# A running state formed in 128x32 column tiles and applied in 32x32 array tiles, with a new written order of steps

## The chip, the core and the metric

The program runs on one core of a Trainium2 chip. TensorE multiplies matrices (PE in the profile, its weight loads PEld), VectorE is DVE, ScalarE is ACT, GpSimd is POOL, and the DMA queues are issued from SP and POOL. The metric is the device time of one launch in microseconds (us), as the median of several runs. Profiled times are of one execution.

## The reference

A batch of 32 rows of 256 tokens goes through three stages. The first is a two-layer tower of width 128 with 8 heads of 16 (below). Its output of width 256 then goes through an attention without softmax (16 heads of 64) and a gated MLP of 768, each added to its input.

```python
# one layer of the tower; H=8 heads, HD=16
q, k, v = (layernorm(x) @ w + b, split into heads); k = k / sqrt(HD)
k, v = causal_conv(filters, k), causal_conv(filters, v)
Z = einsum('bhsd,bhse->bhsde', v, k)
gates = relu(Z.reshape(.., HD*HD) @ gk + gb)**2 + EPS
attn = cumsum(gates * Z, axis=2) / (cumsum(gates, axis=2) + EPS)
o = einsum('bhsd,bhsde->bhse', q, attn); o = o / max(norm(o), EPS)
x = x + o @ ok + ob
x = x + gelu(layernorm(x) @ ff1 + b1) @ ff2 + b2
```

The sum over positions of `gates * Z` is, for each head, a 16x16 matrix that grows along the sequence: v transposed times (gate times k). The kernel cuts the 256 positions into two halves of 128. The second half needs that matrix summed over the whole first half. This is "the running state" here.

## The kernel before, in words

Two batch rows make a group, so there are 16 groups. The tower treats four groups at a time (streams 0 to 3), each in its own buffers, shifted in time against each other, so that a new group enters while three are at later steps. The rest (attention and MLP, called B here) has two streams.

Nothing is looped on the chip: `PLACES_A`, `STARTS_A`, `PLACES_B`, `STARTS_B` and `PREPARE` give every step a number (its place plus the start of its group), all steps are sorted by that number, and each engine issues its own steps in that order and in no other. A step that waits on a semaphore holds all later steps of its engine. The numbers are keys of an order, not times; two groups of the tower stand about 1001 apart. A step is (name, layer or LN number, part); for example `("kv", 1, 0, ...)` is the first half of the keys and values of the second layer. Steps of later groups stand among those of earlier ones.

The attention of one layer of the tower, for one group, in the order of its data:

- `kv`, `conv`, `turn_v`, `gate`: TensorE makes keys and values, convolves them, transposes the values and multiplies them with the gate weights. DVE takes `kv` out (L587) and multiplies in `gate_mul` (L597).
- `gated` (DVE, L605 to L616): sums, bias, square, and at last `gk`, the keys times their gates, laid out in blocks of two heads.
- `state` (PE): for each batch row b, a product of all 128 columns of `vc` (the stationary side) with all 128 columns of the gated keys (L837), 128x128 results of which only the 16x16 blocks on the diagonal are wanted; then two small products with `causal` and `ones` for the sums of the gates (L841, L843). All go into one PSUM bank.
- `state_low` (DVE, L625 to L629): the floor of the norm, and `state`, which is the 128x256 result times `same_head`, a 0/1 matrix that keeps the diagonal blocks.
- `qk` (PE, L856) and `mask` (DVE, L638): the scores in four banks for each pair of positions blocks, times `causal`.
- `av` (PE), parts 0 to 3: the scores with the gated keys, 8 matmuls in 128x32 column tiles (L878). Parts 2 and 3 belong to the second half and first multiply `state` with the queries (L870), one full 128x128 matmul each.
- `norm` (ACT), `sum` (PE, L889), `chain` (DVE, L647 to L665), `unit` (PE, L897), `unit_out` (DVE, L672), `wo` (PE, L903) and `wo_out` (DVE, L678) normalise and project. `f1`, `gelu`, `f2`, `f2_out` are the feed-forward part (L753 to L755, L748, L919, L684).

A layer norm is `stats` (DVE, L562, L567, and L570, the variance), `pow` (POOL, L509), `shift` (DVE, L575), `xn` (ACT, L709), `turn` (PE, L789), `high` (ACT) and `low` (DVE, L581). POOL also does `bias` (x plus the bias of the next projection, L514), `embed` (L504) and `gather` (L479).

A float32 matmul of the program shows as two MATMUL instructions (and two LDWEIGHTS) in the trace. PSUM banks are handed out in the order in which the sorted steps claim them, a ring of 8 in the tower.

Of the kernel before, what the change touches and what calls it, by code (L numbers as in the profile page):

```python
# [10 lines left out]
ALU = mybir.AluOpType  # L11
# [24 lines left out]
PLACES_A = [("embed", 0, 0, 335), ("stats", 0, 0, 506), ("pow", 0, 0, 630), ("shift", 0, 0, 680), ("xn", 0, 0, 757),  # L36
            ("turn", 0, 0, 592), ("high", 0, 0, 809), ("low", 0, 0, 822), ("bias", 0, 0, 1024), ("q", 0, 0, 941),
            ("q_out", 0, 0, 1183), ("kv", 0, 0, 763), ("kv_out", 0, 0, 881), ("kv", 0, 1, 771),
            ("kv_out", 0, 1, 883), ("conv", 0, 0, 841), ("conv_out", 0, 0, 932), ("conv", 0, 1, 859),
            ("conv_out", 0, 1, 945), ("turn_v", 0, 0, 895), ("vT_out", 0, 0, 1131), ("gate", 0, 0, 992),  # L40
            ("gate_mul", 0, 0, 1284), ("gated", 0, 0, 1354), ("state", 0, 0, 1246), ("state_low", 0, 0, 1467),
            ("qk", 0, 0, 960), ("mask", 0, 0, 961), ("qk", 0, 1, 1198), ("mask", 0, 1, 1450), ("av", 0, 0, 1248),
            ("av", 0, 1, 1311), ("av", 0, 2, 1314), ("av", 0, 3, 1336), ("norm", 0, 0, 1583), ("sum", 0, 0, 1399),
            ("chain", 0, 0, 1684), ("unit", 0, 0, 1481), ("unit_out", 0, 0, 1773), ("wo", 0, 0, 1661),
            ("wo_out", 0, 0, 1842), ("stats", 1, 0, 1853), ("pow", 1, 0, 1993), ("shift", 1, 0, 1903),
            ("xn", 1, 0, 1895), ("turn", 1, 0, 1883), ("high", 1, 0, 2048), ("low", 1, 0, 1945),
            ("bias", 1, 0, 2176), ("f1", 0, 0, 1954), ("gelu", 0, 0, 2248), ("f1", 0, 1, 1956), ("gelu", 0, 1, 2271),
            ("f1", 0, 2, 2017), ("gelu", 0, 2, 2359), ("f1", 0, 3, 2060), ("gelu", 0, 3, 2434), ("f2", 0, 0, 2130),
            ("f2", 0, 1, 2151), ("f2", 0, 2, 2212), ("f2", 0, 3, 2229), ("f2_out", 0, 0, 2474),
            ("stats", 2, 0, 2483), ("pow", 2, 0, 2563), ("shift", 2, 0, 2652), ("xn", 2, 0, 2602),  # L50
            ("turn", 2, 0, 2451), ("high", 2, 0, 2720), ("low", 2, 0, 2701), ("bias", 2, 0, 2993), ("q", 1, 0, 2710),
            ("q_out", 1, 0, 2866), ("kv", 1, 0, 2487), ("kv_out", 1, 0, 2731), ("kv", 1, 1, 2587),
            ("kv_out", 1, 1, 2758), ("conv", 1, 0, 2628), ("conv_out", 1, 0, 2764), ("conv", 1, 1, 2633),
            ("conv_out", 1, 1, 2822), ("turn_v", 1, 0, 2673), ("vT_out", 1, 0, 2830), ("gate", 1, 0, 2823),
            ("gate_mul", 1, 0, 2897), ("gated", 1, 0, 2917), ("state", 1, 0, 2891), ("state_low", 1, 0, 2926),
            ("qk", 1, 0, 2838), ("mask", 1, 0, 2911), ("qk", 1, 1, 2872), ("mask", 1, 1, 2920), ("av", 1, 0, 2892),
            ("av", 1, 1, 2894), ("av", 1, 2, 2919), ("av", 1, 3, 2936), ("norm", 1, 0, 3130), ("sum", 1, 0, 2950),
            ("chain", 1, 0, 2959), ("unit", 1, 0, 3035), ("unit_out", 1, 0, 2984), ("wo", 1, 0, 3076),
            ("wo_out", 1, 0, 3312), ("stats", 3, 0, 3338), ("pow", 3, 0, 3337), ("shift", 3, 0, 3444),
            ("xn", 3, 0, 3526), ("turn", 3, 0, 3283), ("high", 3, 0, 3531), ("low", 3, 0, 3483),  # L60
            ("bias", 3, 0, 3772), ("f1", 1, 0, 3358), ("gelu", 1, 0, 3591), ("f1", 1, 1, 3361), ("gelu", 1, 1, 3680),
            ("f1", 1, 2, 3403), ("gelu", 1, 2, 3709), ("f1", 1, 3, 3441), ("gelu", 1, 3, 3758), ("f2", 1, 0, 3414),
            ("f2", 1, 1, 3468), ("f2", 1, 2, 3480), ("f2", 1, 3, 3626), ("f2_out", 1, 0, 3801),
            ("stats", 4, 0, 3801), ("pow", 4, 0, 3781), ("shift", 4, 0, 3854), ("xn", 4, 0, 3882),
            ("turn", 4, 0, 3882), ("high", 4, 0, 3991), ("low", 4, 0, 3934), ("head", 0, 0, 3942),
            ("head_out", 0, 0, 3957), ("head", 0, 1, 3983), ("head_out", 0, 1, 3994), ("idx", 0, 0, 1577),
            ("gather", 0, 0, 1897), ("gather", 0, 1, 1993), ("gather", 0, 2, 3512), ("gather", 0, 3, 3925),
            ("store", 0, 0, 3837)]
STARTS_A = [434, 1435, 2438, 3441, 4443, 5445, 6445, 7448, 8448, 9448, 10450, 11450, 12454, 13455, 14458, 15457]
PLACES_B = [("b_load", 0, 0, 485), ("b_stats", 0, 0, 411), ("b_pow", 0, 0, 346), ("b_xn", 0, 0, 510),  # L70
            ("b_turn", 0, 0, 1053), ("b_high", 0, 0, 1144), ("b_low", 0, 0, 1023), ("b_turn", 0, 1, 1119),
            ("b_high", 0, 1, 1209), ("b_low", 0, 1, 1075), ("rows_high", 0, 0, 429), ("rows_low", 0, 0, 578),
            ("gram", 0, 0, 658), ("gram_high", 0, 0, 787), ("gram_low", 0, 0, 787), ("gram", 1, 0, 723),
            ("gram_high", 1, 0, 887), ("gram_low", 1, 0, 809), ("t1", 0, 0, 760), ("t1_even", 0, 0, 869),
            ("t1_odd", 0, 0, 812), ("t1", 0, 1, 763), ("t1_even", 0, 1, 919), ("t1_odd", 0, 1, 845),
            ("keys", 0, 0, 826), ("keys_out", 0, 0, 947), ("keys", 0, 1, 834), ("keys_out", 0, 1, 974),
            ("r", 0, 0, 988), ("r_high", 0, 0, 1007), ("r_low", 0, 0, 976), ("r", 0, 1, 1015),
            ("r_high", 0, 1, 1059), ("r_low", 0, 1, 1016), ("m", 0, 0, 1036), ("m", 0, 1, 1041), ("m", 0, 2, 1054),
            ("m_high", 0, 0, 1164), ("m_low", 0, 0, 1034), ("attn", 0, 0, 1144), ("attn_out", 0, 0, 1129),
            ("t1", 1, 0, 844), ("t1_even", 1, 0, 1014), ("t1_odd", 1, 0, 941), ("t1", 1, 1, 1000),  # L80
            ("t1_even", 1, 1, 1038), ("t1_odd", 1, 1, 977), ("keys", 1, 0, 1017), ("keys_out", 1, 0, 1119),
            ("keys", 1, 1, 1023), ("keys_out", 1, 1, 1147), ("r", 1, 0, 1060), ("r_high", 1, 0, 1164),
            ("r_low", 1, 0, 1053), ("r", 1, 1, 1097), ("r_high", 1, 1, 1167), ("r_low", 1, 1, 1071),
            ("m", 1, 0, 1126), ("m", 1, 1, 1131), ("m", 1, 2, 1135), ("m_high", 1, 0, 1223), ("m_low", 1, 0, 1107),
            ("attn", 1, 0, 1165), ("attn_out", 1, 0, 1132), ("b_stats", 1, 0, 1143), ("b_pow", 1, 0, 1156),
            ("b_xn", 1, 0, 1210), ("b_turn", 1, 0, 1211), ("b_high", 1, 0, 1367), ("b_low", 1, 0, 1213),
            ("b_turn", 1, 1, 1222), ("b_high", 1, 1, 1380), ("b_low", 1, 1, 1218), ("b_gate", 0, 0, 1515),
            ("b_up", 0, 0, 1624), ("silu", 0, 0, 1724), ("hid", 0, 0, 1744), ("hid_high", 0, 0, 1812),
            ("hid_low", 0, 0, 1923), ("b_gate", 1, 0, 1576), ("b_up", 1, 0, 1728), ("silu", 1, 0, 1780),
            ("hid", 1, 0, 1769), ("hid_high", 1, 0, 1849), ("hid_low", 1, 0, 2004), ("b_gate", 2, 0, 1583),  # L90
            ("b_up", 2, 0, 1762), ("silu", 2, 0, 1791), ("hid", 2, 0, 1955), ("hid_high", 2, 0, 2438),
            ("hid_low", 2, 0, 2057), ("b_gate", 3, 0, 1634), ("b_up", 3, 0, 1843), ("silu", 3, 0, 2001),
            ("hid", 3, 0, 2018), ("hid_high", 3, 0, 2491), ("hid_low", 3, 0, 2077), ("b_gate", 4, 0, 1767),
            ("b_up", 4, 0, 2432), ("silu", 4, 0, 2072), ("hid", 4, 0, 2436), ("hid_high", 4, 0, 2494),
            ("hid_low", 4, 0, 2435), ("b_gate", 5, 0, 1862), ("b_up", 5, 0, 2436), ("silu", 5, 0, 2076),
            ("hid", 5, 0, 2439), ("hid_high", 5, 0, 2498), ("hid_low", 5, 0, 2449), ("down", 0, 0, 2368),
            ("down", 1, 0, 2406), ("down", 2, 0, 2440), ("down", 3, 0, 2447), ("down", 4, 0, 2492),
            ("down", 5, 0, 2499), ("add", 0, 0, 2485), ("add", 1, 0, 2486), ("send", 0, 0, 2488)]
# [130 lines left out]
def token_tower(nc, semaphores, a, h_rows):  # L229
# [1296 lines left out]
```

## Time and profile before

| | us |
|---|---|
| median of 3 runs (lowest, highest) | 2023.23 (2022.75, 2024.51) |
| the profiled execution's own time | 2023.51 |
| its span | 2021.6 |

| engine | busy us | share of the span |
|---|---|---|
| PE | 1854.7 | 92% |
| PEld | 1586.4 | 78% |
| DVE | 1183.7 | 59% |
| ACT | 723.1 | 36% |
| POOL | 443.7 | 22% |

The busy time of PE is modelled, as matmuls are pipelined. In a timeline the first number of a row is the start in us from the start of the span, the second how long the merged instructions took together, "x16" how many they are, and in brackets stands for how long the engine was idle before and who ended that. The tower fills the span up to some 960 us, and B the rest.

### The profile page before, as it was taken

The numbers are of one execution on the slowest core, as the hardware profiler recorded it, in microseconds if no ns is written. First come the engines' busy times: TensorE is split into PE (matmuls) and PEld (weight loads), VectorE is DVE, ScalarE is ACT, GpSimd is POOL, SyncE is SP. The second block draws the span as 40 slices with busy tenths as digits, with TensorE's granted clock in tenths as the row PEclk, the third lists the DMA queues.
The fourth block names the chain that finished last, engine by engine and source line by source line (L and its number), as shares of the span: only waits on it lengthen the run. The fifth ranks groups of instructions, "written<-read, shape, count | busy, mean of one in ns | idle before, by whom it ended". The sixth has DMA issues, their size and how long they took to land.

```text
span 2021.6 us, 41920 instructions
## 1 busy us (share of the span) xinstructions
PE 1854.7 (92%) x17154; PEld 1586.4 (78%) x17154; DVE 1183.7 (59%) x3021; ACT 723.1 (36%) x1448; POOL 443.7 (22%) x393
## 2 busy tenths in 40 slices
PE   2689999999999999977899999999999999999998
PEld 1477778787778788866788888888888888888887
DVE  1468888888888888765644444344344444444443
ACT  1244444444444444442333222322232223222232
POOL 3213333332323222111111221122112211121112
PEclk8789999999999999987899999999999999999999
DMA  4000000000000000002100000000000000000000
GB/s 94 7 4 7 17 17 17 17 18 17 17 16 17 16 14 12 12 32 92 60 2 22 22 22 3 20 22 22 16 7 22 22 22 1 22 22 22 1 22 21
DMA packets 28699, 42.45 MB, mean 21 GB/s; under 512 B 6240, under 2 KB 22112, under 8 KB 28512
## 3 DMA queue, kind: packets, MB, share of 16 engines
q1 hardware_dynamic: 26464, 35.59, 5.5%
q0 software_dynamic: 2048, 4.20, 0.8%
q8 instruction: 138, 2.26, 0.5%
q14 instruction: 49, 0.40, 0.1%
HBM read 23.00 MB, written 16.78 MB: 20 GB/s over the span
## 4 chain that ended last, share of the span: by engine, by line
PE 57%; DVE 28%; issue 6%; POOL 3%; DMA 3%; SPq 1%; ACT 1%; DVEq 0%; POOLq 0%; ACTq 0%
PE ps L1314 11%; PE ps L1316 10%; PE ps L1315 10%; DVE att L638 5%; PE ps L1364 3%; PE ps L1380 3%; DMA h<-h_rows 3%; DVE bxn L1179 3%; PE ps L753 2%; DVE stats L562 2%; DVE bstats L1163 2%; PE ps L811 2%; PE ps L903 2%; PE ps L755 2%; PE ps L754 2%
## 5 line engine op out<-in xcount | busy, mean ns | idle before, releaser
L1153 POOL TENSOR_TENSOR hids_low<-hid,hids_high 128x512 fp32r<-128x512 f32 x96 | 137.8, 1442 | 606.1 <-ACT hids_high L1300 606.0
L509 POOL TENSOR_TENSOR rstd<-var,minus_half 128x4 f32<-128x4 f32 x80 | 83.2, 1040 | 607.0 <-DVE var L570 605.9
L709 ACT ACTIVATE xn<-x,shift,rstd 128x128 f32<-128x128 f32 x320 | 131.6, 484 | 163.0 <-DVE shift L575 162.9
L638 DVE TENSOR_TENSOR att<-ps,causal 128x512 f32<-128x512 f32 x256 | 158.3, 678 | 14.5 <-PE ps L856 14.5
L1314 PE MATMUL ps<-r_high,wq_high 128*128 128x256 f32 x512 | 148.9, 291 | 0.7 <-issue 0.7
L1316 PE MATMUL ps<-r_high,wq_low 128*128 128x256 f32 x512 | 144.8, 283 | 0.0
L1315 PE MATMUL ps<-r_low,wq_high 128*128 128x256 f32 x512 | 144.8, 283 | 0.0
L919 PE MATMUL ps<-w_f,wide 128*128 128x128 f32 x1024 | 130.0, 278 | 0.1
L919 PEld LDWEIGHTS ps<-w_f,wide 128*128 128x128 f32 x1024 | 122.2, 193 | 6.4 <-issue 5.0
L1300 ACT ACTIVATE hids_high<-hid 128x512 fp32r<-128x512 f32 x96 | 59.8, 630 | 146.8 <-PE ps L1316 134.6
L1314 PE MATMUL ps<-wd_high,hids_high 128*128 128x256 f32 x384 | 111.3, 290 | 0.7 <-POOL hids_low L1153 0.7
L1294 ACT ACTIVATE silu<-ps 128x512 f32<-128x512 f32 x96 | 55.4, 596 | 155.3 <-DVE hid L1229 86.3
L1315 PE MATMUL ps<-wd_low,hids_high 128*128 128x256 f32 x384 | 108.5, 283 | 0.0
L1316 PE MATMUL ps<-wd_high,hids_low 128*128 128x256 f32 x384 | 108.5, 283 | 0.0
L748 ACT ACTIVATE wide<-ps,b_f 128x512 f32<-128x512 f32 x128 | 84.5, 685 | 59.8 <-PE ps L755 59.8
L1202 DVE COPY t<-ps 128x512 f32<-128x512 f32 x64 | 44.1, 689 | 104.8 <-PE ps L1316 104.8
L1314 PE MATMUL ps<-wv_high,gram_high 128*128 128x512 f32 x256 | 105.0, 410 | 0.2 <-issue 0.2
L1210 DVE TENSOR_TENSOR r_low<-ps,r_high 128x512 fp32r<-128x512 f32 x128 | 80.9, 684 | 38.4 <-ACT r_high L1278 38.4
L1278 ACT ACTIVATE r_high<-ps 128x512 fp32r<-128x512 f32 x128 | 67.8, 599 | 97.1 <-PE ps L1380 97.1
L1315 PE MATMUL ps<-wv_low,gram_high 128*128 128x512 f32 x256 | 100.1, 391 | 0.0
L1316 PE MATMUL ps<-wv_high,gram_low 128*128 128x512 f32 x256 | 99.8, 390 | 0.0
L1185 DVE TENSOR_TENSOR bxT_low<-ps,bxT_high 128x512 fp32r<-128x512 f32 x64 | 42.8, 689 | 97.2 <-ACT bxT_high L1251 97.2
(354 smaller groups left out, 5055.3 us busy)
## 6 DMA issues: line engine op xcount, KB each, us to landing
h_rows<-h_out SPq DMA_DIRECT2D x16, 512.0 KB, 2.6
h<-h_rows SPq DMA_DIRECT2D x16, 512.0 KB, 3.9
out<-bxn SPq DMA_DIRECT2D x32, 256.0 KB, 2.5
att<-in_filters SPq DMA_DIRECT2D x1, 1024.0 KB, 7.0
emb<-in_embed,idx POOLq DMA_INDIRECT x64
stage<-in_W_vT SPq DMA_DIRECT2D x2, 512.0 KB, 4.8
wo<-in_W_oT SPq DMA_DIRECT2D x1, 1024.0 KB, 6.4
stage<-in_W_q SPq DMA_DIRECT2D x2, 512.0 KB, 6.8
```

The lines of the kernel that those rows point to most:

```text
L509: pool.tensor_tensor(rstd[s][:], var[s][:], minus_half[:], ALU.pow)\
L638: dve.tensor_tensor(masked[:, :, PAIR * g:PAIR * g + PAIR, :], bank("qk", s, l, j, g, t)[:].rearrange("p (n r t) -> p n r t", n=2, r=PAIR) ...
L709: act.activation(xn[s][:, j, :], x[s][:, j, :], ACT.Identity, bias=shift[s][:, j:j + 1], scale=rstd[s][:, j:j + 1]).then_inc(xn_made[s].se ...
L748: act.activation(gl[s][:, j, :], bank("f1", s, l, j, t)[:], ACT.Gelu_apprx_tanh, bias=b_f1[:, l, j:j + 1]).then_inc(gl_made[s].sem, 1)
L919: ins = pe.matmul(out[:, D * j:D * j + D], gl[s][:, f, P * j:P * j + P], w_f2[l][:, f, :], start=(f == 0 and j == 0), stop=(f == FC - 1), ...
L1153: pool.tensor_tensor(hids[1][:, halves, :], hid[:, half, :], hids[0][:, halves, :].bitcast(F32), ALU.subtract).then_inc(hid_low[s].sem, 1)
L1179: ins = dve.tensor_scalar(xn[s][:, j, :], h[s][:, j, :], mv[s][:, j, 0:1], rstd[s][:, j:j + 1], ALU.subtract, ALU.mult)
L1210: dve.tensor_tensor(low, bank("r", s, b, k, t)[:], high.bitcast(F32), ALU.subtract)\
L1278: act.activation(r[0][:, 2 * k:2 * k + 2, :].rearrange("p k n -> p (k n)"), bank("r", s, b, k, t)[:], ACT.Copy).then_inc(r_high[s].sem, 1)
L1314: pe.matmul(out, lhsT[0], rhs[0], start=start, stop=False, **kw)
L1315: pe.matmul(out, lhsT[0], rhs[1], start=False, stop=False, **kw)
L1316: return pe.matmul(out, lhsT[1], rhs[0], start=False, stop=stop, **kw)
```

## The change

The state bank shrinks: for each batch row it holds 128x32 results in place of 128x128. Row block q (partitions 32q to 32q+31, two heads) gets its own 128x32 column tile, with the 32 gated columns of the same two heads, so that only the blocks near the diagonal are formed. The mask is now `parity`, which tells the even head of a pair from the odd. The two gate sums come first in `state`. Where the state is applied, four matmuls in 32x32 array tiles stand in place of one of 128x128.

```diff
-    state = each("state", [P, NB, D])
+    state = each("state", [P, NB, BLOCK])
...
-            dve.tensor_tensor(state[s][:], bank("state", s, l, t)[:, 0:NB * D].rearrange(
-                "p (b d) -> p b d", b=NB), same_head[:].unsqueeze(1).to_broadcast([P, NB, D]),
-                ALU.mult).then_inc(g.sem, 1)
+            dve.tensor_tensor(state[s][:].rearrange("p b (r e) -> p b r e", r=PAIR),
+                              bank("state", s, l, t)[:, 0:NB * BLOCK].rearrange("p (b r e) -> p b r e", b=NB, r=PAIR),
+                              parity[:].unsqueeze(1).unsqueeze(3).to_broadcast([P, NB, PAIR, HD]),
+                              ALU.mult).then_inc(g.sem, 1)
...
-            for b in range(NB):
-                pe.matmul(out[:, D * b:D * b + D], vc[s][:, b, :],
-                          heads[:, PAIRS_A * b:PAIRS_A * b + PAIRS_A], start=(b == 0),
-                          stop=True, skip_group_check=True)
-            z, w = NB * D, NB * HEADS
-            pe.matmul(out[:, z:z + 2 * w], causal[:], gate[s][:], start=False, stop=False,
+            z, w = NB * BLOCK, NB * HEADS
+            pe.matmul(out[:, z:z + 2 * w], causal[:], gate[s][:], start=True, stop=False,
                       skip_group_check=True)
             pe.matmul(out[:, z + w:z + 2 * w], ones[:], gate[s][:, 0:w], start=False, stop=True,
-                      skip_group_check=True).then_inc(p_gate[s].sem, 1)
+                      skip_group_check=True)
+            for b in range(NB):
+                for q in range(PAIRS_A):
+                    rows = slice(BLOCK * q, BLOCK * q + BLOCK)
+                    ins = pe.matmul(out[rows, BLOCK * b:BLOCK * b + BLOCK], vc[s][:, b, rows],
+                                    heads[:, PAIRS_A * b + q], start=True, stop=True, skip_group_check=True)
+            ins.then_inc(p_gate[s].sem, 1)
...
-                pe.matmul(out, state[s][:, b, :], qT_last[s][:, P * b:P * b + P], start=True, stop=False,
-                          skip_group_check=True)
+                for q in range(PAIRS_A):
+                    rows = slice(BLOCK * q, BLOCK * q + BLOCK)
+                    pe.matmul(out[rows, :], state[s][rows, b, :], qT_last[s][rows, P * b:P * b + P], start=True,
+                              stop=False, skip_group_check=True)
```

All five order tables are written anew as well. Most steps keep their neighbours. The keys that change an order inside the repeating part of the tower, before and after (groups 1001 apart before, about 1004 after; a step of a group that entered n groups later adds n times that):

| step | before | after |
|---|---|---|
| `state` 1 and `av` 1,0 | 2891, 2892 | 2917, 2906 |
| `pow` 1, `bias` 2 | 1993, 2993 | 1969, 3047 |
| `bias` 1, `pow` 3, `embed` | 2176, 3337, 335 | 2176, 3119, 314 |
| `bias` 0 | 1024 | 1499 |
| `gate_mul` 1, `shift` 4, `shift` 1 | 2897, 3854, 1903 | 2926, 3918, 1918 |
| `chain` 0, `shift` 0 | 1684, 680 | 1704, 703 |
| `unit` 0, `kv` 1,0 and 1,1, `turn` 0 | 1481, 2487, 2587, 592 | 1654, 2628, 2629, 643 |
| `gate` 0, `f1` 0,2, `unit` 1 | 992, 2017, 3035 | 1092, 2054, 3093 |
| `av` 0,1 and `turn` 3 | 1311, 3283 | 1334, 3352 |
| `norm` 1 and `vT_out` 0 (ACT) | 3130, 1131 | 3196, 1160 |

In B, `b_gate` and `b_up` alternate earlier, `hid_low` 0 comes ahead of `b_pow` and `rows_high` of the next group, and `b_turn` 0 comes ahead of the second half of `keys`. In `PREPARE`, `wk_load` and the first `w_high` and `w_low` come earlier.

## Rows read from the trace of the kernel before

**Rows 1.** Stretches of the span: length, busy time of each engine, clock, DMA.

```profile
100.00:840.00 740.00, 697.07 (x7474) 587.40 (x7470) 614.23 (x1812) 351.86 (x745) 210.42 (x199) 0.99 0.05 15
840.00:1000.00 160.00, 127.77 (x1101) 106.95 (x1102) 93.52 (x247) 58.54 (x112) 19.57 (x17) 0.86 0.17 58
1000.00:2021.00 1021.00, 989.06 (x8293) 860.10 (x8291) 447.76 (x864) 295.38 (x554) 183.37 (x141) 1.00 0.05 17
```

**Rows 2.** Who waited for whom, PE alone, 100 to 850 us.

```profile
PE ps L837 <- DVE gk L616: 19.8, 24, 1.3
PE ps L897 <- DVE sq L665: 9.3, 13, 3.4
PE ps L870 <- DVE state L629: 9.3, 26, 0.4
```

**Rows 3.** Timeline of PE: one period of the tower, from second-layer state to the next.

```profile
508.56 0.71 PE L837 MATMUL ps<-gk,vc 128*128 128x128 f32 x4 [1.04 <-DVE gk L616]
...
529.03 0.71 PE L837 MATMUL ps<-gk,vc 128*128 128x128 f32 x4 [0.64 <-DVE gk L616]
...
530.02 0.64 PE L878 MATMUL ps<-att,gk 128*32 128x128 f32 x16
...
532.15 0.49 PE L870 MATMUL ps<-qT_last,state 128*128 128x128 f32 x2 [0.33 <-DVE state L629]
532.57 0.64 PE L878 MATMUL ps<-att,gk 128*32 128x128 f32 x16
533.14 0.49 PE L870 MATMUL ps<-qT_last,state 128*128 128x128 f32 x2
...
541.65 0.66 PE L897 MATMUL ps<-ident,sq 128*128 128x128 f32 x4 [0.45 <-DVE sq L665]
...
558.50 1.09 PE L789 MATMUL ps<-ident,xn 128*128 128x128 f32 x8
560.63 0.71 PE L837 MATMUL ps<-gk,vc 128*128 128x128 f32 x4 [1.03 <-DVE gk L616]
561.17 0.31 PE L841 MATMUL ps<-gate,causal 128*128 128x32 f32 x2
...
563.68 0.49 PE L870 MATMUL ps<-qT_last,state 128*128 128x128 f32 x2 [0.39 <-DVE state L629]
```

**Rows 4.** Timeline of DVE in the same period, the pieces that the argument uses.

```profile
527.01 0.77 DVE L613 TENSOR_SCALAR gate<-gate 128x32 f32<-128x32 f32 x1
527.81 1.16 DVE L616 TENSOR_TENSOR gk<-kc,gate 128x512 f32<-128x512 f32 x1
...
537.42 1.24 DVE L575 SCALAR_TENSOR_TENSOR shift<-mv,rstd 128x4 f32<-128x4 f32 x1 [1.06 <-POOL rstd L509]
...
551.75 0.76 DVE L570 TENSOR_SCALAR var<-mv 128x4 f32<-128x4 f32 x1
...
554.42 1.77 DVE L575 SCALAR_TENSOR_TENSOR shift<-mv,rstd 128x4 f32<-128x4 f32 x1
...
560.49 2.48 DVE L638 TENSOR_TENSOR att<-ps,causal 128x512 f32<-128x512 f32 x4
```

**Rows 5.** Timeline of POOL in the same period.

```profile
527.02 1.40 POOL L504 TENSOR_TENSOR x<-emb,pos 128x256 f32<-128x256 f32 x2
...
551.20 1.28 POOL L514 TENSOR_TENSOR x<-x,b_o 128x512 f32<-128x512 f32 x1
552.59 1.05 POOL L509 TENSOR_TENSOR rstd<-var,minus_half 128x4 f32<-128x4 f32 x1
...
554.88 1.28 POOL L514 TENSOR_TENSOR x<-x,b_o 128x512 f32<-128x512 f32 x1
```

**Rows 6.** Groups of instructions by line and form: busy us, mean ns, idle before.

```profile
L856 PE MATMUL ps<-wide,vT 32*128 32x256 f32 x1024 | 74.9, 407 | 4.3 <-ACT qT_last L722 4.3
L629 DVE TENSOR_TENSOR state<-ps,same_head 128x256 f32<-128x256 f32 x32 | 13.3, 417 | 0.0
L625 DVE TENSOR_SCALAR floor<-ps 128x32 f32<-128x32 f32 x32 | 5.6, 176 | 0.2 <-PE ps L843 0.2
```

More of the change, by code:

```diff
@@ L33 @@
 GK_SLOTS, ATT_SLOTS = 1, 2
[L36 to L98, printed above, removed]
@@ new lines @@
+STARTS_B = [18514, 19762, 21023, 22288, 23537, 24792, 26041, 27294, 28547, 29798, 31064, 32331, 33585, 34842, 36101,
+            37362]
+PREPARE = [("w_load", 0, 17582), ("w_high", 0, 18188), ("w_low", 0, 18341), ("w_load", 1, 17683),
+           ("w_high", 1, 18345), ("w_low", 1, 18910), ("w_load", 2, 18140), ("w_high", 2, 19197),
+           ("w_low", 2, 19222), ("w_load", 3, 19040), ("w_high", 3, 19375), ("w_low", 3, 19509),
+           ("w_load", 4, 19715), ("w_scale", 4, 19577), ("w_high", 4, 19710), ("w_low", 4, 19640),
+           ("w_load", 5, 20132), ("w_scale", 5, 19633), ("w_high", 5, 19906), ("w_low", 5, 19712),
+           ("w_load", 6, 20659), ("w_scale", 6, 19692), ("w_high", 6, 20038), ("w_low", 6, 20131),
+           ("w_load", 7, 20664), ("w_scale", 7, 19911), ("w_high", 7, 20153), ("w_low", 7, 20178),
+           ("w_load", 8, 20828), ("w_scale", 8, 20221), ("w_high", 8, 20164), ("w_low", 8, 20549),
+           ("w_load", 9, 20887), ("w_scale", 9, 20340), ("w_high", 9, 20624), ("w_low", 9, 20770),
+           ("wk_load", 0, 17765), ("wo_load", 0, 18228)]
@@ L623, in vector @@
             dve.wait_ge(p_gate[s].sem, p_gate[s].at(t, 3 * l + 3))
-            dve.tensor_scalar(floor[s][:], bank("state", s, l, t)[:, NB * D:NB * D + J * HEADS], EPS,
+            dve.tensor_scalar(floor[s][:], bank("state", s, l, t)[:, NB * BLOCK:NB * BLOCK + J * HEADS], EPS,
                               EPS_NORM, ALU.add, ALU.mult).then_inc(g.sem, 1)
```

75 lines of the change are left out of this document (63 added, 12 removed).

## The prediction

> **What bounds the kernel now.** I read the table by stretches first. From 100 to 840 us, where the tower repeats itself, PE is busy 697 of 740 us at full clock and DVE 614 of 740; from 1000 us on PE is busy 989 of 1021 and DVE 448 [rows 1]. So B is bound by PE alone, and its products are not touched. The tower has two engines near their limit, and the question there is which one the other waits for. The list of waits answers: in the tower PE stands 19.8 us for `gk`, 9.3 for `sq` of the norm and 9.3 for `state`, all from DVE [rows 2]. The timeline places them. L837 at 508.56 comes again at 560.63, so a group costs 52.07 us. In that period PE waits 1.03 for the second layer's `gk`, 0.39 for its state, 0.64 for the first layer's `gk`, 0.33 for its state and 0.45 for `sq` [rows 3]. That is 2.84 us of 52. Last I looked at what holds DVE there: instructions that take 0.2 us or less when free take 0.76, 1.24 and 1.77 us [rows 4], and each begins while POOL is inside an add over SBUF and ends as that ends [rows 5]. So PE waits for DVE, and DVE in part for POOL. About 15 of the 16 periods look like this.
>
> **State formed (L837 to L843, 32 times).** Before, from 560.63 to L841 at 561.17 is 0.54 us for four instructions of 128x128, and state as a whole, 529.03 to L878 at 530.02, is 0.99 us [rows 3]. The new one has 16 small instructions in place of the four. The trace has no such form. Upper bound: L878 issues 16 of 128x32 with four times the moving columns from 532.57 to 533.14, 0.57 us. Lower bound: a quarter of it, 0.14, as 32 columns stream in place of 128. I take 0.35, between the two, since a small instruction may not shrink with its columns. That is 0.2 us less PE per state, with ends +0.03 and -0.4. It is worth almost nothing: the PE work of state is over about 1 us before DVE ends the masks of the same layer (560.49 plus 2.48 us) [rows 4], and `state_low` stands behind these masks in DVE's queue. If that cover were gone it would be 0.2 x 32, some 6 us.
>
> **State applied (L870, 64 times).** Two instructions take 532.15 to 532.57, 0.42 us, though 16 narrow ones after them take 0.57 [rows 3]. The new form is 8 instructions in 32x32 tiles, not in the trace. Nearest are L878 (four column tiles, 0.57 for 16, so half of it, 0.29, plus about 0.05 for the entry) and L856 (32-row tiles, 256 columns, mean 407 ns each, yet 1024 of them are busy only 74.9 us together, so row tiles do overlap) [rows 3, 6]. I take 0.34: 0.08 less, 64 times 5 us at most, 0.1 us for each pair on the path. Upper end: if tiles that differ in both row and column do not overlap, 8 times 0.107 plus 0.2 is 1.06 us, 0.64 more each (0.107 is half of 0.42 with half taken off for the change of form).
>
> **Changes of array form.** In the second layer `av` 0 now stands ahead of `state`. Counting the order, the forms change 9 times in place of 6 there, and 7 in place of 8 in the first layer: two more per group. The price by rows: L870 takes 0.42 where two instructions at L837's pace (0.54 for four) would take 0.27 and at the fastest pace 0.21, so 0.15 to 0.2 each. I charge nothing, because those of the second layer fall before the wait for state. *The rule that weighs against the change*: the Trainium skill, TensorEngine Tiling (Array Packing), section Tiling Modes, says that a change of tiling mode drains the array. The 0.42 us agree with it. By the rule, with no cover at all, the sum would be 16 x 0.4, 6 us slower than mine; by the row with its cover, nothing.
>
> **The mask of the state (L629).** 256 elements take 417 ns and 32 take 176 [rows 6], so 1.08 ns an element, and 64 elements take about 210 ns: 0.2 us less. PE waits behind it in both layers (0.39 and 0.33) [rows 3], so both 0.2 count, or 0.4 us a period if nothing else moved.
>
> **The new order.** It is the larger part, step by step for a period, with the numbers of rows 3 to 5.
>
> 1. `pow` 1 goes ahead of `bias` 2. L570 at 551.75 is held by that bias (551.20 plus 1.28) and takes 0.76; free it takes 0.17. It ends 0.6 earlier. The bias then runs after `pow`, from about 553.0 to 554.3. `bias` 0 leaves this place (it was the add at 554.88).
> 2. `shift` 4 and 1 now stand ahead of `gate_mul`. They come up at about 553.3, behind two `kv_out` (four passes of 256 elements, 1.4 us by L629's 0.42 each, a little overlapped [rows 6]), are held by that bias to 554.4, and `gate_mul` (a pass of 512, 0.6 as each of the four in 2.48) ends at 555.1. Before, L575 at 554.42 was held 1.77 us by a gather and the bias behind it, to 556.19. The masks start 1.0 us earlier, and so does `gk`. PE is ready at 559.59 (558.50 plus 1.09): the wait of 1.03 is all but gone. Late next is `state_low` of this layer. With the shorter mask PE applies the state 1.2 earlier, and with 0.1 from the two applications 1.3.
> 3. The price: `bias` 1 now stands between `pow` 3 and `embed`. At 527.01, where L613 and L616 lie, POOL did 1.40 us of `embed`; it will do 1.28 of bias first. L613 is held to 528.3, and L616 (0.69 free) to the end of one half of `embed`, 529.0, or of both, 529.7. So `gk` comes at 529.7 or 530.3, not at 528.97: 0.7 or 1.35 given back. I take 0.7. *Rule*: the Trainium skill, SBUF — State Buffer, on the shared port pair, calls it an exclusive lock for a whole instruction, which a VectorE instruction in a 2-port mode or with two SBUF inputs takes or waits for. The rows above agree. It does not say who wins between the two halves of `embed`; with a loss each time its sum is the 1.35.
> 4. The shorter mask gives 0.2 again and the applications 0.1. PE is at 1.3 - 0.7 + 0.2 + 0.1, less 0.1 for a `shift` that `embed` may hold: 0.8 ahead.
> 5. `chain` goes ahead of `shift` 0, which waited 1.06 for `pow` and was held 1.24 [rows 4]. `unit` goes behind `kv` 1, so the wait of 0.45 for `sq` goes. `kv` 1 needs `low` 20, behind that `shift`. If `bias` 3 holds the shift as before, PE waits about 0.6 there; if not, nothing. So from +0.45 to -0.2; I take -0.05, nearer to the held case, which is the row.
>
> The sum is 0.75 us a period, with ends 0.75 - 0.65 - 0.25 = -0.15 and 0.75 + 0.5 = 1.25. Over 15 periods 11 us, between -2 and +19. `unit` and `gate` of the other layer, `norm` behind `vT_out` and the banks of the ring only move inside PE-bound stretches: nothing. Every bank is claimed after at least as much PE work as before, within a step.
>
> **The change between the stages** (840 to 1000 us, PE busy 128 of 160 at a clock of 0.86 [rows 1]). `w_high` and `w_low` go to places where ACT and DVE were idle; `w_low` 2 now stands ahead of `b_xn` (1.2 us, with slack behind it). Nothing, within 5 us either way. B's repeating part: the waits on `rows_low` stay, because `hid_low` 0 ends before `b_pow` starts. Nothing, within 3 us.
>
> The profiled execution took 2023.51, so 2023.5 - 11 = 2012 us. That execution is 0.3 above the median, which the forecast ignores.
>
> **Rivals.**
>
> - *The given-back case, no change.* POOL's adds hold `gk` by 1.35 and the `shift` again: step 3 at its dear end and step 5 at its low. For it: POOL's work is moved, not lessened, and PE waits at each of these places. Against it: step 2 has its own room of 1 us. -0.15 x 15: 2020 to 2027, 2024.
> - *Slower, by the applied state.* The four 32x32 tiles do not overlap: 0.64 x 4 for a group, of which some 0.3 lies under waits, so 2.3 x 16 = 37, less 11 gained: 2050. Decides from the point where 8 instructions take over 0.6 us. For it: no such tile is in the trace. Against it: column tiles and row tiles each overlap.
> - *Slower, by POOL's adds ahead of `embed`.* If they also hold `gk`'s small instructions one after another, `gk` is 2 us late rather than 0.7: -0.55 a period, 2032. From 1.45 us of delay on it is slower than before.
> - *All of PE's waits go.* 2.84 x 15 = 43 us, 1981, if DVE kept ahead everywhere. Halfway, 2000. Against it: DVE is busy 83% and `gk` of the first layer stays late.
> - *The drains count in full* (the rule above): 2018.
> - *The smaller product does nothing by itself*, and the time is the order's alone: the same 2012 less 5, so 2017; it cannot be told from the forecast by the time, only by runs that do one part.
>
> **How the numbers follow.** Forecast and its neighbours, 2004 to 2019: 0.55 (with the drains and the order alone in it). No change, 2019 to 2027.5: 0.18. Slower by the order: 0.09; by the tiles 0.06. Much faster, below 2004: 0.12. 0.2%, what this kernel's measurement tells from nothing, is 4 us. Faster by more: 0.67; within: 0.18; slower: 0.15. The range leaves about 0.1 on each side: 1998 to 2030.
>
> **What would show it.** In the changed profile the period (L837's successor in `state` to the next) should be 51.3 us; the wait for `gk` in the second layer under 0.2, and in the first layer above 1 us; `state` of DVE about 210 ns; L616's successor still held, its mean at or above 880 ns; L870's block 0.3 to 0.36 us; the B part as long as before. I am wrong if the period is over 52, if the applied state takes over 0.5 us, or if the first layer's `gk` is not late.

## The result, and the profile after

| | before | after |
|---|---|---|
| median of 8 runs each, side by side (lowest, highest), us | 2023.87 (2021.06, 2027.74) | 2029.8 (2027.12, 2032.2) |
| ratio to before, 95% interval | | 1.0026 [1.0014, 1.0037] |
| span of the profiled execution, us | 2021.6 | 2028.1 |

The change makes the kernel slower by 0.26%, 5.9 us. I had forecast 12 us less. Three executions of the experiments below stand far outside the others (two of e5, 2315 and 2351 us at a granted clock of 0.74 and 0.73, and one of e7, 4479 us); they are in the medians given there, but not in the ratios. The stretches (length, busy time of PE, PEld, DVE, ACT, POOL, then clock and DMA) answer to [rows 1]:

```profile
100.00:840.00 740.00, 691.52 (x8244) 578.86 (x8244) 613.94 (x1829) 361.05 (x759) 220.33 (x203) 0.99 0.05 15
840.00:1000.00 160.00, 127.35 (x1106) 104.35 (x1106) 89.54 (x227) 57.12 (x106) 17.04 (x15) 0.81 0.17 58
1000.00:2021.00 1021.00, 993.65 (x8274) 859.38 (x8274) 445.85 (x864) 295.84 (x553) 168.35 (x141) 1.00 0.05 16
```

In the tower PE is less busy (691.5 for 697.1). In B it is busy 4.6 us longer in the same 1021 us, though B's products are the same: their order costs PE something. The waits of PE from 100 to 850 us (total, times, longest) answer to [rows 2]:

```profile
PE ps L875 <- DVE state L629: 21.0, 28, 1.4
PE ps L838 <- DVE gk L616: 16.5, 14, 1.7
PE ps L883 <- issue: 3.1, 12, 0.3
```

The wait for `sq` is gone, and the one for `gk` is left in one layer only (14 times for 24). The wait for the state has more than doubled, from 9.3. The second-layer state in the timeline of PE, to be laid beside [rows 3]:

```profile
553.14 0.64 PE L883 MATMUL ps<-att,gk 128*32 128x128 f32 x16
553.72 0.41 PE L838 MATMUL ps<-gate,causal 128*128 128x32 f32 x2
553.96 0.37 PE L840 MATMUL ps<-gate,ones 128*128 128x16 f32 x2
554.27 0.33 PE L845 MATMUL ps<-gk,vc 128*32 128x32 f32 x16
554.41 0.62 PE L883 MATMUL ps<-att,gk 128*32 128x128 f32 x16
554.97 0.66 PE L824 MATMUL ps<-ident,vc 128*128 128x128 f32 x4
555.87 0.42 PE L875 MATMUL ps<-qT_last,state 32*32 32x128 f32 x8 [0.25 <-DVE state L629]
556.22 0.65 PE L883 MATMUL ps<-att,gk 128*32 128x128 f32 x16
```

Nothing waits ahead of L838 at 553.72. The 16 small products take from 554.27 to 554.41, 0.14 us; the 8 tiles of the application from 555.87 to 556.22, 0.35. Half a period earlier stands the new loss. DVE, then POOL, around the first-layer state:

```profile
519.78 1.28 DVE L613 TENSOR_SCALAR gate<-gate 128x32 f32<-128x32 f32 x1
521.09 1.16 DVE L616 TENSOR_TENSOR gk<-kc,gate 128x512 f32<-128x512 f32 x1
...
522.77 2.47 DVE L639 TENSOR_TENSOR att<-ps,causal 128x512 f32<-128x512 f32 x4
525.17 0.18 DVE L625 TENSOR_SCALAR floor<-ps 128x32 f32<-128x32 f32 x1
525.38 1.25 DVE L628 TENSOR_TENSOR floor<-floor 128x32 f32<-128x32 f32 x1
526.55 0.21 DVE L629 TENSOR_TENSOR state<-ps,parity 128x64 f32<-128x64 f32 x1
```

```profile
519.75 1.27 POOL L514 TENSOR_TENSOR x<-x,b_f 128x512 f32<-128x512 f32 x1
520.98 1.85 POOL L504 TENSOR_TENSOR x<-emb,pos 128x256 f32<-128x256 f32 x2
523.00 1.02 POOL L479 DMA_INDIRECT emb<-in_embed,idx  x1 [0.17 <-issue]
524.32 0.94 POOL L479 DMA_INDIRECT emb<-in_embed,idx  x1 [0.30 <-issue]
525.29 1.27 POOL L514 TENSOR_TENSOR x<-x,b_o 128x512 f32<-128x512 f32 x1
```

L628, 0.19 us when free, starts 0.09 after a bias add and ends with it. PE waits for it:

```profile
526.82 0.42 PE L875 MATMUL ps<-qT_last,state 32*32 32x128 f32 x8 [1.41 <-DVE state L629]
```

With the order tables every step of PE in one trace has its partner in the other. In us from the span's start, after less before: the first-layer `state` of the thirteenth group -8.8, the first `gram` of B -2.6, the second group's `gram` +0.6, the last group's `b_gate` +6.6. So the tower's steady part gains 8.8 (a period of 51.14 in place of 52.12, mean of seven), its end gives back 6.2, the change between the stages 3.2, and B 6.0.

### The profile page after: what moved, and what is told of

Its sections match the earlier page's. It is cut to its first block, busy times and chain, and to the rows that moved or that the text cites. A ratio compares the mean times of both kernels' runs of the same rounds, so it can differ in the third digit from the quotient of the medians.

```text
span 2028.1 us, 43456 instructions
## 1 busy us (share of the span) xinstructions
PE 1855.6 (91%) x17922; PEld 1575.6 (78%) x17922; DVE 1179.2 (58%) x3021; ACT 729.3 (36%) x1448; POOL 433.2 (21%) x393
## 4 chain that ended last, share of the span: by engine, by line
PE 65%; DVE 22%; issue 5%; DMA 3%; POOL 3%; SPq 2%; ACT 1%; DVEq 0%; POOLq 0%; ACTq 0%
PE ps L1319 11%; PE ps L1320 10%; PE ps L1321 10%; DVE att L639 6%; PE ps L754 4%; PE ps L1369 3%; PE ps L1385 3%; DMA h<-h_rows 3%; PE ps L755 3%; PE ps L756 3%; PE ps L924 3%; DVE bxn L1184 3%; PE ps L883 2%; DVE bstats L1168 2%; PE ps L812 2%
## 5 line engine op out<-in xcount | busy, mean ns | idle before, releaser
L1158 POOL TENSOR_TENSOR hids_low<-hid,hids_high 128x512 fp32r<-128x512 f32 x96 | 123.4, 1287 | 767.5 <-ACT hids_high L1305 767.5
L509 POOL TENSOR_TENSOR rstd<-var,minus_half 128x4 f32<-128x4 f32 x80 | 81.7, 1021 | 628.5 <-DVE var L570 628.5
L1319 PEld LDWEIGHTS ps<-r_high,wq_high 128*128 128x128 f32 x512 | 97.9, 191 | 3.1 <-issue 0.9
L1234 DVE TENSOR_TENSOR hid<-silu,ps 128x512 f32<-128x512 f32 x96 | 64.4, 684 | 61.6 <-PE ps L1321 59.1
L1320 PEld LDWEIGHTS ps<-r_low,wq_high 128*128 128x128 f32 x512 | 98.2, 192 | 0.0
```

The lines of the kernel that those rows point to most:

```text
L509: pool.tensor_tensor(rstd[s][:], var[s][:], minus_half[:], ALU.pow)\
L1158: pool.tensor_tensor(hids[1][:, halves, :], hid[:, half, :], hids[0][:, halves, :].bitcast(F32), ALU.subtract).then_inc(hid_low[s].sem, 1)
L1234: dve.tensor_tensor(hid[:, uses.place["hid", s, b, t], :], silu[:, uses.place["silu", s, b, t], :], bank("b_up", s, b, t)[:], ALU.mult).th ...
L1319: pe.matmul(out, lhsT[0], rhs[0], start=start, stop=False, **kw)
L1320: pe.matmul(out, lhsT[0], rhs[1], start=False, stop=False, **kw)
```

## The experiments

All ran beside the kernel before, whose median moved from 2023.1 to 2026.6 us between the sessions, so across sessions the ratio decides, not the median. The columns: ratio to before with its interval; the tower's period (from the fifth group's first-layer `state` to the twelfth's); lead over the profile of before at the thirteenth group's state, at the first and the second `gram`, and at the last `b_gate`, negative when ahead; B's period (from the third group's first `gram` to the fifteenth's). The leads are good to some 0.3 us. Part of a lead comes from the first 160 us, which differ also between kernels with the same tower (+3.7 in e4, whose tower is that of before).

| run | ratio | period | lead | B |
|---|---|---|---|---|
| before | 1 | 52.12 | 0 | 66.39 |
| after | 1.0026 [1.0014, 1.0037] | 51.14 | -8.8, -2.6, +0.6, +6.6 | 66.75 |
| e1 | 0.9951 [0.9937, 0.9964] | 51.58 | -4.9, -6.5, -6.9, -8.3 | 66.26 |
| e2 | 1.0202 [1.0187, 1.0216] | 54.46 | +23.2, +28.6, +30.3, +37.6 | 66.87 |
| e3 | 1.0137 [1.0121, 1.0153] | 51.11 | -10.3, -7.2, -3.1, +27.0 | 68.28 |
| e4 | 1.0051 [1.0039, 1.0063] | 52.13 | +3.7, +7.0, +7.4, +13.4 | 66.79 |
| e5 | 0.9978 [0.9967, 0.9988] | 51.14 | -8.5, -2.4, +1.1, -0.3 | 66.24 |
| e6 | 0.9948 [0.9931, 0.9965] | 49.61 | -27.3, -19.0, -17.3, -9.3 | 66.94 |
| e7 | 0.9997 [0.9985, 1.0008] | 52.01 | +0.7, +4.5, +4.2, +3.0 | 66.27 |
| e8 | 1.0129 [1.0109, 1.0149] | 53.56 | +16.0, +24.2, +27.5, +33.7 | 66.77 |
| e9 | 0.9917 [0.9904, 0.9930] | 49.44 | -25.7, -18.9, -15.4, -16.3 | 66.28 |
| e10 | 1.0018 [1.0009, 1.0027] | 50.53 | -15.8, -7.7, -6.0, +1.3 | 66.90 |
| e11 | 1.0022 [1.0013, 1.0031] | 50.22 | -14.9, -4.9, -1.7, +3.8 | 66.73 |
| e12 | 1.0053 [1.0041, 1.0065] | 53.25 | +17.2, +16.0, +15.6, +11.4 | 66.08 |

**e1: the products without the order.** The new code, and all five tables of before.

> The changed kernel's code (state formed in column tiles, masked by parity, applied in 32x32 tiles) with the orders of the kernel before on every engine. My theory: the new products themselves help and the loss sits in the new order of B and of the change between the stages. The mask of the state is 0.2 us shorter at two places that PE waits behind and the application 0.07 shorter at two, so the tower's period falls from 52.08 to about 51.6, B keeps the length of before, and the time is 2023.9 - 0.5 x 15 = about 2016. Rival (the products do nothing by themselves, all of the tower's 0.93 us a period is the order's): period 52.0, time 2022 to 2024. Rival (the new products carry the loss as well): over 2026.

2013.8 us: the small products by themselves are worth 0.5% here. The tower gains 0.54 a period and B loses nothing.

**e2: the order without the products.** The old code and all tables of after.

> The kernel before with the changed kernel's orders on every engine, the products as they were (full 128x128 state). My theory: what is lost after the tower comes with the order whatever the products are, so from the first gram to the end it takes as long as the changed kernel, 6 us more than before, and about 3 us go at the change between the stages; in the tower the order alone gives 0.93 - 0.5 = about 0.4 us a period, 4 us up to the thirteenth group. Time 2030 to 2036, slower than the changed kernel by about 5. Rival (the loss in B is a late effect of the new products): B as in the kernel before, time about 2024.

2062.6 us. B is as long as in the changed kernel, as expected; the tower is far off, 2.3 us a period slower than before, not 0.4 faster. The waits of PE and then the stretches behind them show why:

```profile
544.46 0.71 PE L837 MATMUL ps<-gk,vc 128*128 128x128 f32 x4 [1.14 <-DVE gk L616]
549.17 0.49 PE L870 MATMUL ps<-qT_last,state 128*128 128x128 f32 x2 [2.01 <-DVE state L629]
```

```profile
546.00:549.00 3.00, 1.16 (x24) 0.71 (x16) 2.97 (x6) 1.38 (x4) 2.40 (x3) 1.00 0.16 44
549.00:552.00 3.00, 2.83 (x37) 1.87 (x38) 2.82 (x14) 0.10 (x1) 0.10 (x1) 0.72 0.00 0
552.00:555.00 3.00, 3.00 (x15) 2.53 (x15) 1.20 (x10) 2.31 (x5) 2.36 (x3) 0.71 0.00 0
555.00:558.00 3.00, 3.00 (x22) 2.72 (x22) 2.68 (x7) 2.17 (x7) 2.68 (x3) 1.00 0.17 48
```

For the 6 us behind the long wait the granted clock is 0.72 and 0.71, so for part of them 1.2 GHz, the lower of its two levels, in place of 2.4; this comes back in each period. Four steps there are longer by 0.65, 0.58, 0.17 and 0.10 than in e11 (below), which has the same products and no such wait: 1.5 us. In the changed kernel the wait is 1.41 and the clock does not fall:

```profile
524.00:527.00 3.00, 1.26 (x16) 0.71 (x13) 2.96 (x7) 1.23 (x3) 2.23 (x3) 1.00 0.18 44
527.00:530.00 3.00, 3.00 (x54) 2.02 (x47) 2.82 (x15) 1.20 (x3) 0.46 (x1) 1.00 0.03 5
```

**e3: `keys` together, first attempt.** Two keys of the changed kernel.

```diff
-("b_turn", 0, 0, 1015)  ("keys", 1, 1, 1087)
+("b_turn", 0, 0, 1083)  ("keys", 1, 1, 1068)
```

> The changed kernel with two steps of B moved in TensorE's order and nothing else: the turn of the next half (128x128 products) no longer stands between r and keys of the second half, and the two keys steps of that half (64x64 products) stand side by side again, so three changes of array form fewer in each group. Theory of form changes: they cost 0.14 us each where PE has nothing to wait for, so B falls by 0.42 x 15 = 6 us and the time from 2029.8 to about 2024. Rival (the loss of 0.42 us a group comes from other moves, of casts on DVE and ACT, or from operands that arrive later): no change, 2029 to 2031.

2050.3 us, wrong by 26. The second `keys` now stood for a cast on DVE (`t1_odd` 1,1) that the changed kernel keeps behind the casts of `r`:

```profile
1509.55 1.15 PE L1369 MATMUL ps<-wk,t 128*64 128x64 f32 x32 [1.66 <-issue]
```

Beside that, `b_turn` was 0.23 shorter and one `m` 0.09: two of the changes of form had indeed gone.

**e4: the kernel before with these two steps placed as in the changed one.**

```diff
-("b_turn", 0, 0, 1053)  ("keys", 1, 1, 1023)
+("b_turn", 0, 0, 1016)  ("keys", 1, 1, 1045)
```

> The kernel before with only these two steps moved in TensorE's order, as the changed kernel has them: the turn between r and the first keys step of the second half, the second keys step behind two m products. Theory of form changes: the tower is untouched and B is longer by 0.42 x 15 = 6 us, time about 2030. Rival (other moves make the loss): 2023 to 2025.

2034.8 us, above the 2030 forecast. From the second `gram` to the last `b_gate` it loses 6.0, as the changed kernel does. The rest of the 13.4 us in its profile was lost in the first 160 us (3.7) and at the tower's end (3.3), where the order is that of before.

**e5: `keys` together, with the cast moved too.** e3, and

```diff
-("t1_odd", 1, 1, 1039)
+("t1_odd", 1, 1, 1010)
```

> The move of e3_keys_together once more, and on DVE the cast of the last t1 of the half moved ahead of the last cast of r, as in the kernel before: in e3 the second keys step stood 1.7 us in each group for that cast, so the number of form changes was not what the time showed. Theory of form changes: the five steps that are longer in the changed kernel (the turn 0.59 in place of 0.36, keys 1.08 and 1.08 in place of 0.98 and 1.03, m 1.53 in place of 1.44) are back at the lengths of before, 0.44 to 0.49 us a group, so 6 to 7 us less than the changed kernel: 2023 to 2024. Rival (the two keys steps wait for another operand, a cast on ACT, when they stand early): the wait of e3 stays in part, 2030 or more.

2022.4 us, just under the 2023 to 2024 forecast; at the last `b_gate` it is 6.9 us ahead of the changed kernel. The mean length of the five steps (start to start of the next, groups 2 to 13 counted from 0) is the proof, for between after and e5 no other step of B differs by over 0.015, nor, but for the last `b_gate` (0.08 less), between before and e4:

```
step        before   after   e4      e5
b_turn 0,0  0.355    0.586   0.586   0.355
keys 1,0    0.982    1.082   1.082   0.981
keys 1,1    1.033    1.081   1.082   1.034
m 0,1       1.440    1.529   1.529   1.440
m 0,2       3.048    3.065   3.065   3.047
```

The sum is 0.49 us a group for three more changes between the 128x128, 64x64 and 128x64 forms (12 for 9 a group by the order), 0.16 each. That the two places cost it is shown both ways. That the change of form is the reason, and not another effect of the neighbour, is read from which steps grew: each of the five has a neighbour of another form where it had one of its own, and no other step has. The rest of B's new order gains: e5 wins 1.4 us over the kernel before from the second `gram` to the last `b_gate`, so the changed kernel loses 15 x 0.49 less 1.4, its 6.0. In the rows (after, then e5) look at the distance from L1333 to the next line, 0.59 and 0.35:

```profile
1496.66 1.09 PE L1385 MATMUL ps<-wo,kvs 64*64 64x256 f32 x16
1497.68 0.66 PE L1333 MATMUL ps<-ident,bxn 128*128 128x128 f32 x4
1498.27 1.15 PE L1369 MATMUL ps<-wk,t 128*64 128x64 f32 x32
1499.35 0.38 PE L1319 MATMUL ps<-r_high,wq_high 128*128 128x256 f32 x1
1499.57 0.28 PE L1320 MATMUL ps<-r_low,wq_high 128*128 128x256 f32 x1
```

```profile
1500.05 0.60 PE L1333 MATMUL ps<-ident,bxn 128*128 128x128 f32 x4
1500.40 0.36 PE L1319 MATMUL ps<-r_high,wq_high 128*128 128x256 f32 x1
```

**e6: POOL's adds in the tower moved.** Three keys of the changed kernel; PE's and DVE's order are untouched.

```diff
-("embed", 0, 0, 314)  ("bias", 0, 0, 1499)  ("bias", 1, 0, 2176)
+("embed", 0, 0, 100)  ("bias", 0, 0, 1640)  ("bias", 1, 0, 2460)
```

> The changed kernel with three steps of POOL moved and nothing else: the embedding's add goes ahead of the power step before it, the bias add of the feed-forward goes behind the gathers, and the bias add that held L628 (1.25 us in place of 0.19) goes behind the power step of the next turn. Theory (POOL's adds, by where they stand, set both waits of the first layer, 1.14 us for gk and 1.41 for state): L628 is back at 0.19 and L613 at 0.18, gk comes at least 1.1 us and the state another 1.1 us earlier, so 1.0 to 2.2 us of the period's 51.15 go and the time is 2000 to 2015. Rival (the adds hold other instructions in their new places and give it back): period within 0.3 of 51.15, time 2025 to 2033.

2016.1 us, just over the 2015 forecast, and 1.54 us a period. The two waits of the first layer (1.14 and 1.41) are gone; 0.69 for `gk` and 0.38 for the state have come up in the second, where the embedding's add now falls:

```profile
638.06 0.64 PE L883 MATMUL ps<-att,gk 128*32 128x128 f32 x16 [0.69 <-DVE gk L616]
640.92 0.42 PE L875 MATMUL ps<-qT_last,state 32*32 32x128 f32 x8 [0.38 <-DVE state L629]
```

The bias adds fall on `chain`, whose small steps are held instead, but PE hardly waits for `sq` there, and it waits some 0.3 us in most periods for the cast L581 behind them. L628 takes 0.24 us in the mean (0.59 in the changed kernel). The end of the tower gives back 8.3 of the 27.3 us, again.

**e7: e1 with a long mask.** L629 works on 256 elements again, with the new products (mean 418 ns for 217).

> e1_products_alone (new products, orders of before) with the mask of the state made as long as before: 256 elements, of which only the 64 that the products use have a meaning; the products are not touched. It separates the two parts of the 0.54 us a period that e1 won. If the shorter mask on DVE is what counts, as my forecast had it (0.2 us at each of two waits), the period goes from 51.58 back to about 52.0 and the time from 2013.8 to about 2020. If PE's shorter steps count (state 0.70 in place of 1.00 twice, the applications 0.92 in place of 0.99 four times, 0.88 us in all, part of it given back as waits), the period stays at 51.6 to 51.7 and the time at 2014 to 2016.

2026.1 us beside a kernel before at 2026.6, so no gain is left (ratio 0.9997), where 2020 was forecast. The period is 52.01, as forecast: the 0.43 us that e1 won over it are the mask's. The products alone, 52.12 to 52.01, give 0.1, although each state is 0.30 us shorter on PE and each application 0.07; PE gets to its waits sooner.

**e8: e2 with a short mask.** The old products with 64 elements in L629, the rest of the state zero.

> e2_order_alone (old products, new orders) with the mask of the state cut to 64 elements; the rest of the state is left at zero, so the applied state is not the reference's, and all products run in full. In e2 PE waits 2.01 us for the state in one piece each period, after 1.14 for gk, and the granted clock of the next 6 us is 0.71; in the changed kernel the wait is 1.41 and the clock stays at 1.00. Theory (the order alone is slow because the long wait lets the clock fall): the wait is 1.8 us; if that is short enough, the clock stays at 1.00, the period falls from 54.46 by 0.2 plus 1.6 to about 52.6, time about 2035; if it still falls, 54.2 and 2058. Rival (the mask's length is what makes the wait in the next layer too): period below 52.2, time under 2030.

2054.5 us. The wait is 1.8 in each period, but the clock falls in some only, so the run lies between the two branches. From 329 to 341 us it stays at 1.00; from 382 to 388 it is 0.79. From the fifth group's first-layer state to the twelfth's, the two periods in which it stays last 52.3 us and the five in which it falls 54.0 to 54.3. So a fall costs 1.7 us, seen inside one kernel at one length of wait, and it accounts for about half of the 0.9 us that the mean period gains on e2. The mask alone does not rescue this order.

**e9: e5 and e6 together.** The keys of both.

> The moves of e5_keys_together_2 (TensorE in B) and of e6_pool_moved (POOL in the tower) in one kernel, on top of the changed kernel. If the two losses are independent, as their places 900 us apart suggest, the period is 49.6 as in e6, a group of B is 0.50 us shorter as in e5, and the time is 2016.1 - 7.3 = 2009, with some 3 us either way from how the stages meet: 2005 to 2012. Rival (a faster tower comes to the change between the stages too early for the weights' loads and waits there): 2014 to 2016.

2006.4 us, 17 us below the kernel before and the best of all. The two repairs add up: at the last `b_gate` e5 is 6.9 and e6 15.9 us ahead of the changed kernel, and e9 22.9. The ratios give 0.48% and 0.78% against 1.09%, the same within their intervals.

**e10: one bias add moved.** `bias` 0 alone, 1499 to 1640.

> The changed kernel with one instruction per group moved, POOL's bias add that held L628; the other two moves of e6 are left out. Theory (POOL's add makes the wait for state by itself): L628 falls from 1.25 to 0.19 us in the first layer, the wait for state from 1.41 to about 0.35, the wait for gk stays at 1.14, and the period falls by 1.06 to 50.1; time 2029.8 - 10 to 13 = 2017 to 2020. Rival (only the three moves together help, since DVE is late for gk in any case): period above 50.8, time over 2026.

L628 is back at 0.19, yet the wait for the state only falls to 0.75, since `state_low` then stands behind the masks; and the add holds a step of `chain`. The period falls by 0.62, not 1.06. The time is 2025.9 us, not 2017 to 2020: besides the smaller gain per period the tower's end gives back 8.1 and B loses 7.3. It lies between the theory and the rival (over 2026); that the add makes part of the wait by itself stands, with a smaller price.

**e11: e2 with the POOL moves of e6.**

> e2_order_alone (old products, new orders, 54.46 us a period) with the three POOL moves of e6. Theory of the clock: in e2 the two waits of 1.14 and 2.01 us within 5 us bring the granted clock to 0.72 for the 6 us behind them; with the moves both waits are under 0.8, the clock stays at 1.00, and the period falls by the waits and by the 1.6 us of slow steps, to 50.5 (that of e6 and 0.88 us more of PE work in the state's products): time 2016 + 0.9 x 15 = about 2030, 32 us less than e2. Rival (the old products are slow in this order for another reason, such as operands that come late for the longer state): the moves give what they gave in e6, 1.5 us a period, and the time is 2035 to 2042 or more.

2026.5 us: 36 us less than e2 from three keys of POOL, 4.2 us a period where the same move gave 1.54 with the new products. PE's longest wait in a period is now 0.69, and the clock from 500 to 580 us is 1.00 (it falls once, at 684 to 688 us). Compared with e6, the old products cost 0.61 a period when PE waits little.

**e12: forecast steps 1 and 2 by themselves.** The kernel before with three keys of POOL.

```diff
-("gather", 0, 0, 1897)  ("gather", 0, 3, 3925)  ("bias", 2, 0, 2993)
+("gather", 0, 0, 1700)  ("gather", 0, 3, 3728)  ("bias", 2, 0, 3006)
```

> The kernel before with POOL's order alone changed at the place where DVE's shift was held 1.77 us: the two gathers stand a step earlier, and the power step of the second layer goes ahead of the bias add of the feed-forward. It tests steps 1 and 2 of the forecast by themselves, and what the tower's end does. Theory: the hold of 1.77 us goes, the wait of 1.03 us for gk in the second layer falls under 0.3, and the period is 51.2 to 51.5 in place of 52.08; from the thirteenth group on, where the gathers end, the kernel before has 51.05 anyway, so the new one gains nothing more there. B and the change between the stages are those of before. Time 2023.2 - 0.75 x 12 = about 2014 (2012 to 2017). Rival (the bias add holds the next instruction instead, and PE waits as long): 2021 to 2025.

2033.9 us, a miss: 1.13 us a period slower. The order I had made puts two bias adds in a row behind one gather, and the shift is held longer than before:

```profile
568.33 2.94 DVE L575 SCALAR_TENSOR_TENSOR shift<-mv,rstd 128x4 f32<-128x4 f32 x1
```

```profile
567.69 1.02 POOL L479 DMA_INDIRECT emb<-in_embed,idx  x1 [0.18 <-issue]
568.74 2.50 POOL L514 TENSOR_TENSOR x<-x,b_o 128x512 f32<-128x512 f32 x2
```

It does not isolate steps 1 and 2, for `bias` 0, which leaves this place in the changed kernel, stayed. What it shows is the price of an add that lands wrongly. From the thirteenth group on it neither gains nor loses (+17.2, +16.0).

## Why the prediction was wrong

**The period came out, the waits did not.** It is 51.14 for 51.3 forecast, and many pieces are as told. The wait for `gk` of the second layer is gone, that of the first is 1.14 (over 1 forecast); L629 takes 215 ns (210); L616 935 from 100 to 840 us (at least 880); the application 0.35 (0.34). The state formed takes 0.14 and not 0.35, the lower bound, and e7 finds 0.1 a period for both products by themselves. The mask is worth 0.43 (0.4). But the gain was to come from PE waiting less, and PE does not wait less. Its waits over ten periods, 166 to 685 us, before and then after:

```profile
PE ps L837 <- DVE gk L616: 16.7, 20, 1.0
PE ps L870 <- DVE state L629: 7.1, 20, 0.4
PE ps L897 <- DVE sq L665: 4.6, 9, 0.8
```

```profile
PE ps L875 <- DVE state L629: 18.0, 21, 1.4
PE ps L838 <- DVE gk L616: 11.4, 10, 1.1
PE ps L883 <- issue: 2.9, 11, 0.3
```

With 0.9 for `h_out` the kernel before has 29 us of them and the changed one 32. One cause was missed: I had not followed `bias` 0, of which I only said that it leaves its place. It lands on L628, so the first layer waits 1.41 for the state, not about 0.1. Against it stands that the 0.45 for `sq` went at no price, where step 5 had a loss of 0.05. What fell is PE's own time between its waits, from some 49.2 us a period to 48.0. In e1 (products alone) and in one period of e11 (order, with POOL's moves) it is 48.6, so both parts shorten it. I had put the state formed at nothing and the applications at 0.2 a period. Which steps the order shortens stays open. So the agreement of the period is in part luck.

**One step that failed is the sentence on B**, "Nothing, within 3 us". It decides the sign, for at B's second `gram` the two kernels are level (+0.6). B loses 6.0, and e4 and e5 put and remove it with two steps' places (e5 with a cast's). I knew that `b_turn` 0 moves ahead of the second `keys`, I had the price from L870's row, 0.15 to 0.2 for a change of form, and weighed it in the tower, where I charged nothing because waits covered it. In B, which I had myself called bound by PE alone, I counted no forms. Three more a group, 0.15 to 0.2 each, 15 groups: 7 to 9 us, and the forecast would have been 2020, still 10 under what was measured. The rule of the Trainium skill, TensorEngine Tiling (Array Packing), section Tiling Modes, that a change of tiling mode drains the array, agrees with 0.16 us per change here. The runs time the change; they do not show what the array does in it.

**The other is the count of 15 periods**, "Over 15 periods 11 us", and in us it is the larger. The lead grows for some nine periods only. The kernel before runs at 51.05 from the thirteenth group on, without any change. PE no longer waits there for `gk` of the second layer, since a gather fetches for the group four later and the last four groups issue none; the hold of [rows 4] goes with them (L575 means 695 ns from 166 to 685 us, 572 from 685 to 840). I had taken that hold for a constant. In the changed kernel the adds come earlier as the gathers go, and one falls into `chain` (L659, DVE, then POOL), for which PE waits 1.03 at 741.50:

```profile
737.34 2.03 DVE L659 TENSOR_TENSOR yy<-yy,mh 128x32 f32<-128x32 f32 x1
...
740.76 0.68 DVE L581 TENSOR_TENSOR xT0l<-ps,xT0h 128x512 fp32r<-128x512 f32 x1
```

```profile
736.97 1.02 POOL L479 DMA_INDIRECT emb<-in_embed,idx  x1 [0.18 <-issue]
738.03 1.28 POOL L514 TENSOR_TENSOR x<-x,b_f 128x512 f32<-128x512 f32 x1
```

Together the end gives back 6.2 of the 8.8 won, so the tower gains 2.6 in place of the 11 that I had summed over all periods. Of the 18 us between forecast and time, 8.4 are the tower's, 3.2 come from the change between the stages and 6.0 from B. All three of my signs of being wrong (period over 52, applied state over 0.5, first `gk` not late) lay in the repeating tower, and none of them came.

**The change between the stages** cost 3.2, inside the 5 that I allowed. Which of its moves does it stays open: the kernels with the new tables lose 1.7 to 4.1 there and those with the old ones -0.3 to 0.4, but e4 shows that the stretch just ahead varies by 3 with the same order. A mixture of old and new tables was not tried, because in one the engines can wait for each other.

**The rivals.** The given-back case (2024) and "slower by POOL's adds ahead of `embed`" (2032) both named POOL's adds, and neither happened as told: the first layer's wait for `gk` grew by 0.5 (0.64 to 1.14), near the 0.7 that I took. The sum of the given-back case was also wrong: -0.15 x 15 makes 2026, not 2024. The order alone (2017) was put as a rival with the products idle; e2 shows the opposite, for the order alone is 2% slower. The effects don't add: by the periods, products -0.54, order +2.34, both -0.98. That leaves 2.8 us a period that only the combination saves. The clock is 1.5 to 1.7 of it: with the old products the wait for the state is 2.01 us and the clock falls in each period, with the new it is 1.41 and the clock stays. The shorter wait is another 0.6. That the length of the wait decides is argued, for at 1.8 (e8) the clock falls in some periods and not in others.

## What to carry to other kernels

- Count the changes of array form wherever PE is the bound, above all in stages whose products are untouched and only reordered.
- When an add on POOL moves, follow it to where it lands and read which DVE instruction stands there; e6 and e12 are the same kind of edit, and one gained 1.5 us a period where the other lost 1.1.
- When a period comes out as forecast, add up the waits as well: here they had not fallen, and the period had.
- A gain per period holds as long as its cause: look at the first and last periods of the trace before for one in which the wait is gone by itself.

## What was not expected of the hardware

Three things. Sixteen matmuls of 128x32 in column tiles with 32 moving columns take 0.14 us together, 9 ns each, a quarter of what the same number with 128 moving columns takes (L883, 0.56). The granted clock falls within one period of 54 us and comes back in it: with waits of 1.14 and 2.01 us close together it is at 0.72 for 6 us, with 1.14 and 1.41 it stays at 1.00, and with 1.14 and 1.8 (e8) it falls in some periods only, at 1.7 us each time. And a hold takes in even one of the smallest instructions, L613, a TENSOR_SCALAR from SBUF to SBUF (0.18 free, 1.28 under an add), while the four masks, which read PSUM, kept their 2.47 us through two gathers (522.77 to 525.24).
